# Attention over head pairs: both parts of the values in one stationary operand, halves of the result added on VectorE

## The chip, the cores and the metric

The kernel runs on one core of a Trainium2 chip. The metric is the device time of one execution in microseconds, as the median of several runs. In the profile PE is TensorE's matmuls and PEld its weight loads, DVE is VectorE, ACT is ScalarE, POOL is GpSimd, SP is SyncE, which here issues all transfers.

## The reference

Two layers, each an attention and a feed-forward part, work on 16 batches of 256 tokens with 512 features. Only the attention of the first layer is touched:

```
q = (x @ Wq).reshape(B, N, HEADS, DIM_HEAD)          # 16 heads of 64
out    = attend(q, ctx_txt @ Wk,    ctx_txt @ Wv)    # context rows 0..76
out_ip = attend(q, ctx_img @ Wk_ip, ctx_img @ Wv_ip) # context rows 77..255
return (out + out_ip) @ Wo + bo
# attend: softmax(q k^T / 8) @ v, for each head
```

Here x is the normalized input. The two softmaxes run over different columns of one 256x256 score matrix, and since their results are added, one product of the probabilities (both parts scaled by their own sums) with all 256 value rows gives out + out_ip.

## The kernel before

All products are made from float32r operands in two parts: a high part, and a low part that is what the high part leaves of the float32 value. `product` (lines 186 to 192) issues three matmuls: high x high, high x low and low x high.

The changed function is `attend_pairs`. It works through N = 128 head pairs (16 batches x 8 pairs). It is a software pipeline written out as Python loops: each engine has its own list, and in step s of the list it does its share of several pairs at different stages. The lists are strictly in order; semaphores tie them together. In step s, TensorE does:

- `scores(s)`: eight matmuls of 128x256 into the score tile `sc[s % 2]`, two banks with four blocks (two heads x two query tiles);
- `turn(s - 2)`: eight transposes of the probabilities into `tp`;
- `turn_output`, in one step of four: four transposes of a finished, normalized output tile, into the score tile of the pair before;
- `values(s - 3)`: for each of two heads and two key tiles a `product` into `vq[:, 0]`, twelve matmuls of 128x256. The stationary operand `vs` is 128 columns wide, of which one head's values fill 64 and zeros the others, so that both heads add up in one tile of 128 rows;
- `queries(s + 3)`: twelve matmuls of 128x256 into `vq[:, 1]`, the other half of the same bank;
- `project_out`: six matmuls of 128x512 for two pairs of an output tile, `LAG_O` steps behind; in one step of four a bias matmul comes ahead of them (line 1013).

ScalarE makes the exponentials (`exps`, line 910, in two groups of columns: 77 text and 179 image), the high part of the transposed probabilities (`turned_high`, line 923), of the keys (`keys_high`, line 917), and of outputs and queries in one go (`high_parts`, lines 929 and 933). VectorE finds the row maxima (`largest`, line 802), the sums (`totals`, line 808) and their reciprocals, and the low parts of probabilities (`turned_low`, line 819), outputs and queries (`low_parts`, lines 825 and 827). For each finished output tile, one in four steps, it adds the residual (`output`, line 853) and takes the statistics (lines 833 to 837). GpSimd scales the probabilities (`normalize`, line 773), makes the keys' low part (line 760) and places both parts of the values into `vs` (`place_values`, lines 753 and 755). SyncE's queue loads keys and values and stacks the queries' parts (`stack_q`), four transfers a pair.

## Time and profile before

| | |
|---|---|
| median of 3 runs | 3418.91 us (3418.05 to 3422.42) |
| profiled execution, span | 3417.2 us |
| TensorE busy over the span | 3209.3 us (94%) |
| VectorE, ScalarE, GpSimd busy | 1912.3, 1553.2, 780.6 us |
| `attend_pairs` | about 455 to 1280 us of the span |

The changed part takes a quarter of the span. For it one reads the busy time of each engine inside that stretch, not over the whole span, then the timeline of single steps, and then the list of who waited for whom. Busy time counts overlapping instructions once: an engine's next instruction often starts before the last has ended, so what one adds to a full list is its distance from start to start, which is less than its own length.

### The profile page before, as it was taken

Reading aid. Unit: us, or ns where it says so; the run is one execution under the profiler, and the core shown is the slowest. Engines: PE = TensorE matmul, PEld = TensorE weight load, DVE = VectorE, ACT = ScalarE, POOL = GpSimd, SP = SyncE. Lnnn points to the kernel's source line nnn. Section 1 sums busy time; section 2 is a strip of 40 time slices with the busy share of each in tenths; the row PEclk is TensorE's granted clock in tenths of the full one; section 3 lists DMA queues with packets and bytes.
Section 4 is the critical chain, followed back from the end, with each engine's and each line's share of the span. In section 5 each row is a group of like instructions: output and inputs, shape, how many; then the busy total and the mean of one; then the engine's idle time right before and its main releaser. Section 6 shows DMA issues by size and latency. Waiting matters only on the chain. (4 is left out here: it accounts for less than half of the span.)

```text
span 3417.2 us, 51469 instructions
## 1 busy us (share of the span) xinstructions
PE 3209.3 (94%) x17304; PEld 2753.0 (81%) x17304; DVE 1912.3 (56%) x3294; ACT 1553.2 (45%) x2948; POOL 780.6 (23%) x1138
## 2 busy tenths in 40 slices
PE   7999979999999988999996888997979999999998
PEld 6989969999999986887875576886857888888886
DVE  3244558888888874556888996554753222222211
ACT  3122247777777753335766786654731111111110
POOL 0000047777777750000000200002710000000000
...
GB/s 186 125 250 235 212 184 146 164 163 159 156 157 160 154 96 239 191 175 188 216 226 222 195 275 229 160 161 161 259 117 74 37 35 19 22 37 38 31 25 13
DMA packets 370164, 503.48 MB, mean 147 GB/s; under 512 B 58940, under 2 KB 237420, under 8 KB 366032
## 3 DMA queue, kind: packets, MB, share of 16 engines
...
q8 instruction: 127, 2.08, 0.3%
...
## 5 line engine op out<-in xcount | busy, mean ns | idle before, releaser
L2571 DVE SCALAR_TENSOR_TENSOR lf_hT<-lf_hb,lf_hT 128x512 fp32r<-128x512 f32 x128 | 88.6, 692 | 571.4 <-ACT lf_hT L2647 571.4
L2647 ACT ACTIVATE lf_hT<-lf_hb 128x512 fp32r<-128x512 f32 x128 | 76.6, 599 | 669.1 <-PE lf_py L192 639.6
L910 ACT ACTIVATE at_prob<-at_sc,at_nm 128x77 f32<-128x77 f32 (+1 forms) x1024 | 292.7, 382 | 3.4 <-DVE at_nm L802 3.4
L773 POOL TENSOR_TENSOR at_prob<-at_prob,at_rec 128x308 f32<-128x308 f32 (+1 forms) x256 | 261.6, 1044 | 136.8 <-DVE at_rec L815 136.8
L802 DVE TENSOR_REDUCE at_nm<-at_sc 128x4 f32<-128x308 f32 (+1 forms) x256 | 164.7, 685 | 80.2 <-PE at_sc L965 80.0
L190 PE MATMUL lf_hb<-lf_xT,lf_w 128*128 128x512 f32 x512 | 204.5, 400 | 1.3 <-DVE lf_hT L2571 1.3
L192 PE MATMUL lf_hb<-lf_xT,lf_w 128*128 128x512 f32 x512 | 203.6, 398 | 0.0
L192 PE MATMUL lf_py<-lf_w,lf_hT 128*128 128x512 f32 x512 | 203.4, 397 | 0.0
L190 PE MATMUL lf_py<-lf_w,lf_hT 128*128 128x512 f32 x512 | 203.2, 397 | 0.0
L191 PE MATMUL lf_hb<-lf_xT,lf_w 128*128 128x512 f32 x512 | 203.1, 397 | 0.0
L191 PE MATMUL lf_py<-lf_w,lf_hT 128*128 128x512 f32 x512 | 202.7, 396 | 0.0
L923 ACT ACTIVATE at_pT<-at_tp 128x1024 fp32r<-128x1024 f32 x128 | 131.4, 1027 | 155.7 <-PE at_tp L975 155.7
L2500 POOL TENSOR_SCALAR lf_var<-lf_mv 128x1 f32<-128x1 f32 x32 | 7.4, 230 | 717.6 <-DVE lf_mv L2523 717.6
L190 PE MATMUL pg_bank<-qu_xs,qg_wg 128*128 128x512 f32 x384 | 153.2, 399 | 16.4 <-DVE qu_xs L1396 16.4
L760 POOL TENSOR_TENSOR at_ks<-at_kr,at_ks 128x512 fp32r<-128x512 f32 x128 | 165.0, 1289 | 9.4 <-ACT at_ks L917 9.4
L190 PE MATMUL dn_py<-qf_wd,dn_om 128*128 128x512 f32 x384 | 150.8, 393 | 16.0 <-DVE dn_om L1917 16.0
L808 DVE TENSOR_REDUCE at_sums<-at_prob 128x4 f32<-128x308 f32 (+1 forms) x256 | 162.5, 676 | 0.0
L190 PE MATMUL at_vq<-at_xT,xo_Wq 128*128 128x256 f32 x512 | 146.6, 286 | 13.9 <-DMA at_xT<-xn_parts 11.9
L190 PE MATMUL pu_bank<-qu_xs,qu_wu 128*128 128x512 f32 x384 | 150.8, 393 | 8.5 <-SPq L1270 5.7
L190 PE MATMUL at_vq<-at_pT,at_vs 128*128 128x256 f32 x512 | 154.8, 302 | 0.0
L819 DVE TENSOR_TENSOR at_pT<-at_tp,at_pT 128x1024 fp32r<-128x1024 f32 x128 | 152.7, 1193 | 2.8 <-ACT at_pT L923 2.7
L191 PE MATMUL pg_bank<-qu_xs,qg_wg 128*128 128x512 f32 x384 | 150.7, 392 | 0.0
...
## 6 DMA issues: line engine op xcount, KB each, us to landing
at_kr<-k_rows SPq DMA_DIRECT2D x256, 128.0 KB, 2.9
at_qs<-at_qst SPq DMA_DIRECT2D x512, 64.0 KB, 2.1
...
```

What stands on the lines that cost most here:

```text
L190: pe.matmul(out, lh, rh, start=start, stop=False, **kw)
L191: pe.matmul(out, lh, rl, start=False, stop=False, **kw)
L192: return pe.matmul(out, ll, rh, start=False, stop=stop, **kw)
L760: pool.tensor_tensor(ks[:, n % NK, :, 1, :], kr[:, n % NKR], ks[:, n % NK, :, 0, :].bitcast(F32), ALU.subtract).then_inc(k_low, 1)
L773: ins = pool.tensor_tensor(prob[:, i, :, lo:hi], prob[:, i, :, lo:hi], rec[:, z, g, :].unsqueeze(2).broadcast_to([P, 2 * NTE, hi - lo]), A ...
L802: ins = dve.tensor_reduce(nm[:, n % 2, g, :], sc[n % 2][:, :, lo:hi], AX_X, ALU.max, negate=True)
L808: dve.tensor_reduce(sums[:, z, g, :], prob[:, i, :, SEG[g][0]:SEG[g][1]], AX_X, ALU.add).then_inc(sum_done, 1)
L819: dve.tensor_tensor(pT[:, n % 2, 1], tp[:], pT[:, n % 2, 0].bitcast(F32), ALU.subtract).then_inc(pt_done, 1)
L910: ins = act.activation(prob[:, i, m, lo:hi], sc[n % 2][:, m, lo:hi], ACT.Exp, bias=nm[:, n % 2, g, m:m + 1])
L923: act.activation(pT[:, n % 2, 0], tp[:], ACT.Copy).then_inc(pt_hi, 1)
L2571: dve.scalar_tensor_tensor(hT[:, i, 1, :], hb[i][:], 0.0, hT[:, i, 0, :].bitcast(F32), ALU.max, ALU.subtract).then_inc(h_done, 1)
L2647: act.activation(hT[:, m % 2, 0, :], hb[m % 2][:], ACT.Relu).then_inc(h_hi, 1)
```

## The change

- `vs` becomes `[P, NVP, NTE, 2, 2, DH]`: for a head and a key tile, 64 columns of high parts and 64 of low parts lie side by side, and are one stationary operand of 128 columns. `values` issues, for each head and key tile, two matmuls with it, against the high and the low part of the probabilities: eight instead of twelve. Rows 0 to 63 of the result hold the products with the high part of the values, rows 64 to 127 those with the low part (low x low among them, which was left out before). No zeros are kept any more, and their memset goes.
- The result goes to half of a score tile (`attended(s)`, the first two blocks of `sc[(s + 1) % 2]`), one block of 256 columns for each head. ScalarE copies rows 64 to 127 to `corr` (`corrections`), VectorE adds them to rows 0 to 63 and writes `osum`, head 0 to partitions 0 to 63 and head 1 to 64 to 127 (`halves_summed`).
- From `osum` ScalarE makes the outputs' high part (`outputs_high`) and GpSimd the low part (`outputs_low`), one step later than before.
- The values' high part is made by ScalarE (`values_high`), the low part by GpSimd in one instruction (`values_low`).
- Queries have a bank of their own (`qb`) and come first in TensorE's step. `scores` and `values` wait for `o_summed`, and `values` also for the exponentials of the pair before, whose tile they write.
- `LAG_O` grows from 8 to 9, and the lists of ScalarE, VectorE and GpSimd have a new order.

The core of the diff:

```diff
     NTE = S // P
     N = B * NPAIR
-    LAG_T, LAG_V, LEAD_Q, LAG_P = 2, 3, 3, 2
+    LAG_T, LAG_V, LEAD_Q = 2, 3, 3
     LEAD_K, LEAD_KH, LEAD_KL = 5, 3, 2
-    LAG_O = NPAIR
+    LAG_H, LAG_S = 1, 4
+    LAG_O = NPAIR + 1
...
-        vs = ph.sb("vs", [P, NVP, 2, NTE, 2, P], F32R)
+        vs = ph.sb("vs", [P, NVP, NTE, 2, 2, DH], F32R)
...
+        corr = ph.sb("corr", [DH, 2, S])
+        osum = ph.sb("osum", [P, 2, S])
...
-        vq = ph.ps("vq", [P, 2, S])
+        qb = ph.ps("qb", [P, 2 * S])
...
+        def attended(s):
+
+            return sc[(s + 1) % 2][:, 0:NTE, :]
...
-                    if 0 < s < N and s % 2 == 0:
-                        load_v(s // 2)
+                    if 0 < s + 1 < N and s % 2:
+                        load_v((s + 1) // 2)
...
-                def place_values(n, part):
+                def values_low(n):
                     g, l = n // 2, n % 2
-                    if part == 0:
-                        pool.wait_ge(v_ready[g % 2], 16 * (g // 2 + 1))
-                        if n >= NVP:
-                            pool.wait_ge(vq_full, v_count(n - NVP))
-                    else:
-                        pool.wait_ge(v_high, n + 1)
-                    for h in range(2):
-                        lo = DH * h
-                        to, src = vs[:, n % NVP, h, :, :, lo:lo + DH], vr[:, g % 2, :, l * P + lo:l * P + lo + DH]
-                        if part == 0:
-                            ins = pool.tensor_copy(to[:, :, 0, :], src)
-                        else:
-                            ins = pool.tensor_tensor(to[:, :, 1, :], src, to[:, :, 0, :].bitcast(F32), ALU.subtract)
-                    ins.then_inc(v_high if part == 0 else v_placed, 1)
+                    pool.wait_ge(v_high, n + 1)
+                    pool.tensor_tensor(vs[:, n % NVP, :, :, 1, :], vr[:, g % 2, :, l * P:(l + 1) * P].rearrange("p k (h d) -> p k h d", d=DH),
+                                       vs[:, n % NVP, :, :, 0, :].bitcast(F32), ALU.subtract).then_inc(v_placed, 1)
+
+                def outputs_low(n):
+                    pool.wait_ge(o_hi, n + 1)
+                    pool.tensor_tensor(oT[:, n % NO, 1, :], osum[:, n % 2, :], oT[:, n % NO, 0, :].bitcast(F32), ALU.subtract).then_inc(o_low, 1)
...
-                    if 0 <= s - LAG_P < N:
-                        place_values(s - LAG_P, 0)
                     if 0 <= s + LEAD_KL < N:
                         keys_low(s + LEAD_KL)
-                    if 0 <= s - LAG_P < N:
-                        place_values(s - LAG_P, 1)
                     if 0 <= s - 1 < N:
                         normalize(s - 1)
+                    if 0 <= s - LAG_S < N:
+                        outputs_low(s - LAG_S)
+                    if 0 <= s - LAG_H < N:
+                        values_low(s - LAG_H)
...
-                def low_parts(s):
-                    n, m = s - LAG_V, s + LEAD_Q
-                    dve.wait_ge(vq_hi, s + LEAD_Q + 1)
-                    if 0 <= n < N:
-                        ins = dve.tensor_tensor(oT[:, n % NO, 1, :], vq[:, 0, :], oT[:, n % NO, 0, :].bitcast(F32), ALU.subtract)
-                    if m < N:
-                        ins = dve.tensor_tensor(qst[:, m % NQS, 1, :], vq[:, 1, :], qst[:, m % NQS, 0, :].bitcast(F32), ALU.subtract)
-                    ins.then_inc(vq_done, 1)
+                def halves_summed(s):
+                    n = s - LAG_V
+                    dve.wait_ge(corr_out, n + 1)
+                    if n >= 2:
+                        dve.wait_ge(o_low, n - 1)
+                    for h in range(2):
+                        ins = dve.tensor_tensor(osum[DH * h:DH * h + DH, n % 2, :], attended(s)[0:DH, h, :], corr[:, h, :], ALU.add)
+                    ins.then_inc(o_summed, 1)
+
+                def queries_low(m):
+                    dve.wait_ge(q_hi, m + 1)
+                    dve.tensor_tensor(qst[:, m % NQS, 1, :], qb[:, 0:S], qst[:, m % NQS, 0, :].bitcast(F32), ALU.subtract).then_inc(q_done, 1)
...
+                    if out_tile(s - 1):
+                        output(*out_tile(s - 1))
+                    if 0 <= s - 1 < N:
+                        totals(s - 1, 0)
+                        totals(s - 1, 1)
+                        reciprocals(s - 1)
+                    if out_tile(s - 3):
+                        row_maximum(*out_tile(s - 3))
                     if 0 <= s < N:
                         largest(s)
-                    if 0 <= s - 1 < N:
-                        totals(s - 1, 0)
-                    if 0 <= s - 1 < N:
-                        totals(s - 1, 1)
-                        reciprocals(s - 1)
-                    if out_tile(s - 1):
-                        output(*out_tile(s - 1))
+                    if s + LEAD_Q < N:
+                        queries_low(s + LEAD_Q)
+                    if 0 <= s - LAG_V < N:
+                        halves_summed(s)
                     if out_tile(s - 2):
                         offset(*out_tile(s - 2))
                     if 0 <= s - LAG_T < N:
                         turned_low(s - LAG_T)
-                    if out_tile(s - 3):
-                        row_maximum(*out_tile(s - 3))
-                    if s < N + LAG_V:
-                        low_parts(s)
                     if out_tile(s - 1):
...
-                def high_parts(s):
-                    n, m = s - LAG_V, s + LEAD_Q
-                    act.wait_ge(vq_full, s + LEAD_Q + 1)
-                    if 0 <= n < N:
-                        ins = act.activation(oT[:, n % NO, 0, :], vq[:, 0, :], ACT.Copy)
-                    if m < N:
-                        if m >= NQS:
-                            act.wait_ge(q_ready[(m - NQS) % NQ], 64 * ((m - NQS) // NQ + 1))
-                        ins = act.activation(qst[:, m % NQS, 0, :], vq[:, 1, :], ACT.Copy)
-                    ins.then_inc(vq_hi, 1)
+                def values_high(n):
+                    g, l = n // 2, n % 2
+                    act.wait_ge(v_ready[g % 2], 16 * (g // 2 + 1))
+                    if n >= NVP:
+                        act.wait_ge(v_full, n - NVP + 1)
+                    act.activation(vs[:, n % NVP, :, :, 0, :], vr[:, g % 2, :, l * P:(l + 1) * P].rearrange("p k (h d) -> p k h d", d=DH), ACT.Copy
+                                   ).then_inc(v_high, 1)
+
+                def corrections(s):
+                    n = s - LAG_V
+                    act.wait_ge(v_full, n + 1)
+                    if n:
+                        act.wait_ge(o_summed, n)
+                    act.activation(corr[:], attended(s)[DH:P], ACT.Copy).then_inc(corr_out, 1)
+
+                def outputs_high(n):
+                    act.wait_ge(o_summed, n + 1)
+                    act.activation(oT[:, n % NO, 0, :], osum[:, n % 2, :], ACT.Copy).then_inc(o_hi, 1)
+
+                def queries_high(m):
+                    act.wait_ge(q_full, m + 1)
+                    if m >= NQS:
+                        act.wait_ge(q_ready[(m - NQS) % NQ], 64 * ((m - NQS) // NQ + 1))
+                    act.activation(qst[:, m % NQS, 0, :], qb[:, 0:S], ACT.Copy).then_inc(q_hi, 1)
...
+                    if 0 <= s - LAG_S < N:
+                        outputs_high(s - LAG_S)
+                    if s + LEAD_Q < N:
+                        queries_high(s + LEAD_Q)
+                    if 0 <= s + LEAD_KH < N:
+                        keys_high(s + LEAD_KH)
                     if 0 <= s - LAG_T < N:
                         turned_high(s - LAG_T)
+                    if 0 <= s - LAG_V < N:
+                        corrections(s)
+                    if 0 <= s - LAG_H < N:
+                        values_high(s - LAG_H)
                     if out_tile(s - 3):
                         turned_output(*out_tile(s - 3), s)
                     if 0 <= s < N:
                         exps(s, 0)
-                    if 0 <= s + LEAD_KH < N:
-                        keys_high(s + LEAD_KH)
-                    if s < N + LAG_V:
-                        high_parts(s)
+                        exps(s, 1)
                     if out_tile(s - 2):
                         normalized(*out_tile(s - 2))
-                    if 0 <= s < N:
-                        exps(s, 1)
...
+                    if n > LAG_V:
+                        pe.wait_ge(o_summed, n - LAG_V)
...
-                def values(n):
+                def values(s):
+                    n = s - LAG_V
                     pe.wait_ge(v_placed, n + 1)
                     pe.wait_ge(pt_done, n + 1)
+                    pe.wait_ge(exp_done, 2 * min(s, N))
+                    if n >= 2:
+                        pe.wait_ge(o_summed, n - 1)
                     for h in range(2):
                         for k in range(NTE):
-                            ins = product(pe, vq[:, 0, :], (vs[:, n % NVP, h, k, 0, :], vs[:, n % NVP, h, k, 1, :]),
-                                          (pT[:, n % 2, 0, k, h * S:(h + 1) * S], pT[:, n % 2, 1, k, h * S:(h + 1) * S]),
-                                          h == 0 and k == 0, h == 1 and k == NTE - 1)
-                    return ins
+                            for part in range(2):
+                                ins = pe.matmul(attended(s)[:, h, :], vs[:, n % NVP, k, h, :, :].rearrange("p a d -> p (a d)"),
+                                                pT[:, n % 2, part, k, h * S:(h + 1) * S], start=k == 0 and part == 0, stop=k == NTE - 1 and part == 1)
+                    ins.then_inc(v_full, 1)
...
+                    if n:
+                        pe.wait_ge(q_done, n)
...
-                        ins = product(pe, vq[:, 1, :], (wq[:, 0, lo:lo + P], wq[:, 1, lo:lo + P]), (xT[:, b % 2, 0, k, :], xT[:, b % 2, 1, k, :]),
+                        ins = product(pe, qb[:, 0:S], (wq[:, 0, lo:lo + P], wq[:, 1, lo:lo + P]), (xT[:, b % 2, 0, k, :], xT[:, b % 2, 1, k, :]),
                                       k == 0, k == KD - 1)
-                    return ins
+                    ins.then_inc(q_full, 1)
...
-                        ins = pe.transpose(sc[(s + 1) % 2][:, k * P // S, k * P % S:k * P % S + P],
+                        ins = pe.transpose(sc[(s + 1) % 2][:, NTE + k * P // S, k * P % S:k * P % S + P],
...
-                            pe.wait_ge(vq_done, v_count(n))
+                            pe.wait_ge(o_low, n + 1)
...
+                    if s + LEAD_Q < N:
+                        queries(s + LEAD_Q)
...
-                    if s < N + LAG_V:
-                        if s > FIRST:
-                            pe.wait_ge(vq_done, s + LEAD_Q)
-                        if 0 <= s - LAG_V:
-                            ins = values(s - LAG_V)
-                        if s + LEAD_Q < N:
-                            ins = queries(s + LEAD_Q)
-                        ins.then_inc(vq_full, 1)
+                    if 0 <= s - LAG_V < N:
+                        values(s)
```

In TensorE's list, at a plain step of the steady part, stands before (the three rows of `at_vq<-at_pT` come four times, then those of `at_vq<-at_xT` four times, then the projection):

```order
L965 MATMUL at_sc<-at_ks,at_qs 128x256 x8
L975 MATMUL at_tp<-ident,at_prob 128x128 x8
L190 MATMUL at_vq<-at_pT,at_vs 128x256
L191 MATMUL at_vq<-at_pT,at_vs 128x256
L192 MATMUL at_vq<-at_pT,at_vs 128x256
```

and now (ahead of these rows the three query rows come four times, the projection behind them twice):

```order
L190 MATMUL at_qb<-at_xT,xo_Wq 128x256
L191 MATMUL at_qb<-at_xT,xo_Wq 128x256
L192 MATMUL at_qb<-at_xT,xo_Wq 128x256
L984 MATMUL at_sc<-at_ks,at_qs 128x256 x8
L994 MATMUL at_tp<-ident,at_prob 128x128 x8
L1007 MATMUL at_sc<-at_pT,at_vs 128x256 x8
L190 MATMUL at_pj<-xo_Wo,at_oT 128x512
```

The queries moved ahead of the scores, and eight value matmuls into `at_sc` stand where twelve into `at_vq` did.

VectorE's list, one plain step; `at_sc0` and `at_sc1` are the two score tiles. Before:

```order
L802 TENSOR_REDUCE at_nm<-at_sc1 128x4 x2
L808 TENSOR_REDUCE at_sums<-at_prob 128x4 x2
L815 RECIPROCAL at_rec<-at_sums 128x8
L819 TENSOR_TENSOR at_pT<-at_tp,at_pT 128x1024
L825 TENSOR_TENSOR at_oT<-at_vq,at_oT 128x256
L827 TENSOR_TENSOR at_qst<-at_vq,at_qst 128x256
```

Now:

```order
L801 TENSOR_REDUCE at_sums<-at_prob 128x4 x2
L808 RECIPROCAL at_rec<-at_sums 128x8
L795 TENSOR_REDUCE at_nm<-at_sc0 128x4 x2
L825 TENSOR_TENSOR at_qst<-at_qb,at_qst 128x256
L820 TENSOR_TENSOR at_osum<-at_sc1,at_corr 64x256 x2
L812 TENSOR_TENSOR at_pT<-at_tp,at_pT 128x1024
```

The totals of the pair before moved ahead of the maxima, the queries' low part ahead of the probabilities' low part, and the two additions stand between them.

ScalarE's list, one plain step. Before:

```order
L910 ACTIVATE at_prob<-at_sc0,at_nm 128x179 x4
L923 ACTIVATE at_pT<-at_tp 128x1024
L910 ACTIVATE at_prob<-at_sc1,at_nm 128x77 x4
L917 ACTIVATE at_ks<-at_kr 128x2x256
L929 ACTIVATE at_oT<-at_vq 128x256
L933 ACTIVATE at_qst<-at_vq 128x256
```

Now:

```order
L940 ACTIVATE at_oT<-at_osum 128x256
L946 ACTIVATE at_qst<-at_qb 128x256
L915 ACTIVATE at_ks<-at_kr 128x2x256
L921 ACTIVATE at_pT<-at_tp 128x1024
L936 ACTIVATE at_corr<-at_sc0 64x512
L928 ACTIVATE at_vs<-at_vr 128x4x64
L908 ACTIVATE at_prob<-at_sc1,at_nm 128x77 x4
L908 ACTIVATE at_prob<-at_sc1,at_nm 128x179 x4
```

The copy of the transposed probabilities moved from ahead of the exponentials' text part to the middle of the step, the two groups of exponentials stand together at its end, and behind the probabilities' copy come the new copies of corrections and values.

## Rows read from the trace of the kernel before

**Rows 1.** The page's first line: the profiled execution.
```profile
span 3417.2 us, 51469 instructions
```

**Rows 2.** Busy us and instructions of PE, PEld, DVE, ACT, POOL; PEclk, DMA, GB/s.
```profile
700.00:800.00 100.00, 100.00 (x759) 95.73 (x758) 81.84 (x153) 73.14 (x202) 75.69 (x117) 1.00 0.54 158
```

**Rows 3.** Timeline of PE in one step: start, us long, what, how many.
```profile
804.42 0.40 PE L190 MATMUL at_pj<-xo_Wo,at_oT 128*128 128x512 f32 x1
...
805.81 1.11 PE L965 MATMUL at_sc<-at_ks,at_qs 128*128 128x256 f32 x8
806.76 1.04 PE L975 MATMUL at_tp<-ident,at_prob 128*128 128x128 f32 x8
807.55 0.36 PE L190 MATMUL at_vq<-at_pT,at_vs 128*128 128x256 f32 x1
807.75 0.28 PE L191 MATMUL at_vq<-at_pT,at_vs 128*128 128x256 f32 x1
...
809.06 0.28 PE L190 MATMUL at_vq<-at_xT,xo_Wq 128*128 128x256 f32 x1
...
812.11 1.11 PE L965 MATMUL at_sc<-at_ks,at_qs 128*128 128x256 f32 x8
```

**Rows 4.** Waits, 600 to 1200 us: who for whom, sum, times, longest.
```profile
POOL at_prob L773 <- DVE at_rec L815: 103.2, 72, 1.9
DVE at_nm L802 <- PE at_sc L965: 64.3, 72, 0.9
...
DVE at_oT L825 <- ACT at_qst L933: 33.8, 72, 0.6
```

**Rows 5.** Timeline of DVE in a step with an output tile.
```profile
806.96 1.29 DVE L802 TENSOR_REDUCE at_nm<-at_sc 128x4 f32<-128x308 f32 x2 [0.89 <-PE at_sc L965]
...
809.59 0.64 DVE L853 TENSOR_TENSOR at_y<-at_pj,at_y 128x512 f32<-128x512 f32 x1
810.14 1.22 DVE L819 TENSOR_TENSOR at_pT<-at_tp,at_pT 128x1024 fp32r<-128x1024 f32 x1
811.39 0.42 DVE L825 TENSOR_TENSOR at_oT<-at_vq,at_oT 128x256 fp32r<-128x256 f32 x1
811.74 0.41 DVE L827 TENSOR_TENSOR at_qst<-at_vq,at_qst 128x256 fp32r<-128x256 f32 x1
812.07 0.68 DVE L833 BATCH_NORM_STATS2 at_st<-at_y 128x6 f32<-128x512 f32 x1
...
813.30 1.28 DVE L802 TENSOR_REDUCE at_nm<-at_sc 128x4 f32<-128x308 f32 x2
```

**Rows 6.** Timeline of ACT, two stretches of the steady part.
```profile
804.90 0.38 ACT L933 ACTIVATE at_qst<-at_vq 128x256 fp32r<-128x256 f32 x1
805.16 1.32 ACT L910 ACTIVATE at_prob<-at_sc,at_nm 128x179 f32<-128x179 f32 x4
...
821.14 0.59 ACT L901 ACTIVATE at_xt<-at_sc 128x512 f32<-128x512 f32 x1
821.62 0.98 ACT L910 ACTIVATE at_prob<-at_sc,at_nm 128x77 f32<-128x77 f32 x4
822.45 0.67 ACT L917 ACTIVATE at_ks<-at_kr 128x512 fp32r<-128x512 f32 x1
```

**Rows 7.** Groups of POOL, 600 to 1200 us: busy us, mean ns, idle before.
```profile
L760 POOL TENSOR_TENSOR at_ks<-at_kr,at_ks 128x512 fp32r<-128x512 f32 x97 | 125.0, 1289 | 0.0
...
L755 POOL TENSOR_TENSOR at_vs<-at_vr,at_vs 128x128 fp32r<-128x128 f32 x192 | 84.4, 461 | 0.0
...
L753 POOL CAST at_vs<-at_vr 128x128 fp32r<-128x128 f32 x192 | 50.9, 294 | 0.0
```

**Rows 8.** Timeline of PE in the first steps: scores and transposes of one step.
```profile
485.36 1.12 PE L965 MATMUL at_sc<-at_ks,at_qs 128*128 128x256 f32 x8
486.70 1.09 PE L975 MATMUL at_tp<-ident,at_prob 128*128 128x128 f32 x8 [0.23 <-POOL at_prob L773]
...
490.51 1.12 PE L965 MATMUL at_sc<-at_ks,at_qs 128*128 128x256 f32 x8
```

21 lines of the change are left out of this document (8 added, 13 removed).

## The prediction

> **What bounds the kernel now.** I read the busy shares of each engine by stretch first. In the attention stage TensorE is busy for all of 100 us in 100, at granted clock 1.00, while VectorE has 82, GpSimd 76 and ScalarE 73 [rows 2]. Next comes the timeline of TensorE: a step (one head pair) begins with its scores, and the next scores begin 6.30 us later (805.81 to 812.11), with no idle time between them [rows 3]. The waits of 600 us in the steady part name the other engines as waiting, never TensorE [rows 4]. So a TensorE column removed here is time removed, as long as the others keep up. They are what has to be costed.
>
> That step has a bias matmul, which every fourth one has; of 128x512 each costs 0.23 ((805.81 - 804.42)/6), so a plain step is 6.07 us. Another one of four has four output transposes, 0.4 us by the (807.55 - 806.76)/8 = 0.1 of the others [rows 3]. That makes 6.07 + 0.63/4 = 6.23 us on average. By this, VectorE has 0.818 x 6.23 = 5.10 us of work in a step, ScalarE 0.731 x 6.23 = 4.56, GpSimd 0.757 x 6.23 = 4.72.
>
> **TensorE.** The twelve value matmuls (two heads, two key tiles, three products) become eight: one stationary operand holds 64 columns of high and 64 of low parts, and gets the two parts of the probabilities. A further matmul of 128x256 costs 0.12 us start to start: from 807.75 to 809.06 there are eleven, 0.119 each [rows 3]. Four fewer are 0.476 us a step, and 128 steps give **61.0 us**. Bounds of the new form: its output goes to a score bank instead of vq, but the score matmuls, which write there, take (806.76 - 805.81)/8 = 0.119 too. I take that. The order queries, scores, transposes, values, projection has as many changes of kind as before, so I cost the move at nothing. The new step is 6.23 - 0.48 = 5.75 us.
>
> **ScalarE.** It loses nothing and gains two copies. The correction copy (64x512 out of PSUM) is nearest to the turned output, 128x512 out of PSUM: 0.59 us long, 0.48 before the next starts. Half the partitions could halve it, at best 0.24. The high part of the values (128x256, SBUF) is nearest to the keys' copy, 128x512 in 0.67 [rows 6], and to the queries' copy of 256 columns, 0.26 start to start [rows 6]: I take 0.30, at worst 0.67. The other copies keep their size. Sum 4.56 + 0.48 + 0.30 = 5.34, bounds 5.1 and 5.8: over TensorE's 5.75 only at the worst end.
>
> **VectorE.** It loses the output's low part, 0.35 start to start (811.39 to 811.74), and gains two additions of 64x256 from PSUM and SBUF. The nearest row is that same subtraction, 0.42 long, 0.35 apart; half the partitions might cost half, 0.18 [rows 5]. I take 0.35 each, as the time of the rows goes with the columns: sum 5.10 - 0.35 + 0.70 = 5.45. If they and the instruction behind them get no overlap, it is 5.10 - 0.35 + 0.84 + 0.10 = 5.69; at half the cost, 5.10. All are under 5.75, the upper one by 1%.
>
> [...] The second addition writes from partition 64 on, and the turned_low behind it from 0 on. [...] No row here shows an output that starts at 64. [...]
>
> **GpSimd and the queue.** GpSimd loses two casts (50.9/96 = 0.53 a pair) and two low parts (84.4/96 = 0.88) [rows 7] and gains two subtractions of 128x256, each half of the keys' 1.29 [rows 7]: 4.72 - 1.41 + 1.30 = 4.61, and 5.07 if each costs what the old pair did. It is no bound, and its longest step, the scaling of the probabilities, feeds a transposition two steps later. On SyncE's queue only the load of values moves, by one step; its wait, for values placed a step before, is met by then. stack_q waits for the queries' low part as before, and its result is needed three steps later.
>
> **The new waits.** (a) The values now use the score bank of the pair before, so scores(s+1) wait for halves_summed(s). Behind the last value matmul come 0.2 us until its result is seen, the copy 0.6 [rows 6], two additions 0.84 [rows 5] and handoffs of 0.1, together about 1.75. TensorE has the projection (1.40) and the twelve query matmuls (1.43) to do meanwhile, 2.83 [rows 3]: slack 1.1. (b) queries(s+3) begin the step and wait for the previous queries' low part, which on VectorE stands behind totals, reciprocal and largest. In a plain step the values end at 4.2 us after the step's start, the correction copy at 5.05, the additions at 5.9, turned_low (1.1, 810.14 to 811.39 less its wait [rows 5]) at 7.0. The exponentials, which follow ScalarE's two new copies, run from 5.25 to 7.4 (0.83 + 1.3 [rows 6]); then come totals and reciprocal to 8.5, largest to 9.75 (with the first totals the three take 2.63, 806.96 to 809.59 [rows 5]) and the low part to 10.15. TensorE wants it at 11.3, slack 1.1. After a step with statistics (1.23 from 812.07 to 813.30 [rows 5]) it comes at 11.3 and is wanted at 11.4. That is the tightest place, at 0.1 us, once in four steps. (c) turn(s-1) waits for turned_low(s-2): done at 7.1, wanted at 8.0, and late by about the same in the step after the statistics. I cost all three at nothing; their cover is TensorE's own work, and every 0.1 us of missing cover costs 32 x 0.1 = 3.2 us at (b).
>
> **Start and end.** In the first steps there is no projection, and a step takes 5.15 us (485.36 to 490.51), TensorE waiting for GpSimd's scaling [rows 8]. There the removed matmuls give nothing: five pairs x 0.48 = 2.4 us off the gain. LAG_O + 1 takes one pair's projection (1.40) out of step 8, which becomes 5.15 instead of 5.60, and puts it behind the last values: 1.40 - 0.45 = 0.9 more. Together 3.3 us lost.
>
> **Sum.** 61.0 - 3.3 = 57.7 us gained. Against the profiled span of 3417.2 us [rows 1] that is 3359.5; the median of the runs lies 1.7 above that span, so **3361 us**.
>
> **The rivals.**
> 1. VectorE is late at (b) and (c) after each statistics step. For it: slack 0.1 there, and its waits for ScalarE's copies, 33.8 us in 96 steps [rows 4]. Against it: three of four steps have a microsecond to spare. If 0.5 us is missing a time, 32 x 0.5 = 16 us: 3377.
> 2. VectorE bounds every step. Its upper sum 5.69 plus the 0.35 a step that it now waits for ScalarE (33.8/96) is 6.04, a gain of 0.19 x 128 = 24 less 3: 3398. It needs both at their worst.
> 3. The other side: the lists lock into one ring. Values(s), correction copy, values' copy, both exponentials, totals with reciprocal and largest, queries' low part, additions, and scores, transposes and values two steps on are 0.6 + 0.3 + 0.8 + 1.3 + 2.6 + 0.4 + 0.8 + 2.7, with handoffs 10 us over two steps, against 11.5 that TensorE gives them. It costs time from 12.5 on, the old two steps: the VectorE work of a tile (output 0.64, statistics 1.23 [rows 5]) would have to fall into the ring each time, and its waits for scores (64.3/96 = 0.67 a step [rows 4]) stay as well. Then a step is 5.69 + 0.35 + 0.67 = 6.7, 128 x 0.47 = 60 us slower: 3479.
> 4. The change doesn't do what it says: the new matmuls take 0.179 each, as long as twelve at 0.119. Then 3419 + 3 = 3422. Only the score matmuls speak, and against it.
>
> **How the numbers follow.** Forecast (3355 to 3369) 0.63; first rival (3369 to 3386) 0.18; second (3386 to 3411) 0.09; a small remainder within 0.2% of before, rival 4 among it, 0.04; slower by the ring 0.06. A difference under 0.2% (7 us) is one that these runs can't tell from none. The range has to hold 0.8 and takes in the forecast, the first rival and the lower part of the second: 3355 to 3394. Faster by over 0.2%: 0.63 + 0.18 + 0.09 = 0.90; same 0.04; slower 0.06.
>
> **What would show it.** In the profile after: eight value matmuls a pair at 0.12 us start to start; 100 us in 100 for TensorE from about 510 us on; 5.6 us from scores to scores in plain steps and 5.75 on average; no wait of TensorE's query matmuls for VectorE; VectorE near 95% and ScalarE near 93%. The sum is wrong if TensorE has idle time in front of its queries or transposes once in four steps (rival 1), in each step (rival 2), or in front of its scores, ended by the additions (rival 3).

## The result and the profile after

The changed kernel takes **3376.44 us** (median of 4 runs, 3373.63 to 3377.83) where the kernel before, run beside it, took 3420.66 (4 runs, 3418.05 to 3425.37): ratio 0.9871, 95% interval 0.9859 to 0.9883, 44 us less. The forecast was 3361 with a range of 3355 to 3394; its own narrow case ended at 3369. So direction and range held. The narrow case did not: of the 57.7 us expected, 44.2 came by the medians run side by side. The profiled execution's span fell from 3417.2 [rows 1] to 3375.4, by 41.8, so there 15.9 are missing. From here on a pair is numbered 0 to 127, and scores(5) are the score matmuls of pair 5.

The page's first line, as [rows 1]:

```profile
span 3375.4 us, 51188 instructions
```

The stretch of [rows 2], in the changed kernel (busy us and instructions of PE, PEld, DVE, ACT, POOL; then granted clock, DMA share, GB/s):

```profile
700.00:800.00 100.00, 100.00 (x745) 94.46 (x744) 94.98 (x182) 94.20 (x249) 83.28 (x91) 1.00 0.59 174
```

TensorE still has no idle time there, at granted clock 1.00. VectorE and ScalarE went from 82 and 73 to 95 and 94. One step of TensorE, as [rows 3], with the start of the step behind it:

```profile
801.89 1.12 PE L984 MATMUL at_sc<-at_ks,at_qs 128*128 128x256 f32 x8
...
803.64 1.19 PE L1007 MATMUL at_sc<-at_pT,at_vs 128*128 128x256 f32 x8
804.67 0.39 PE L190 MATMUL at_pj<-xo_Wo,at_oT 128*128 128x512 f32 x1
...
806.08 0.39 PE L190 MATMUL at_qb<-at_xT,xo_Wq 128*128 128x256 f32 x1
806.30 0.28 PE L191 MATMUL at_qb<-at_xT,xo_Wq 128*128 128x256 f32 x1
...
807.61 1.12 PE L984 MATMUL at_sc<-at_ks,at_qs 128*128 128x256 f32 x8
...
813.65 1.12 PE L984 MATMUL at_sc<-at_ks,at_qs 128*128 128x256 f32 x8
...
819.25 1.12 PE L984 MATMUL at_sc<-at_ks,at_qs 128*128 128x256 f32 x8
...
825.08 1.12 PE L984 MATMUL at_sc<-at_ks,at_qs 128*128 128x256 f32 x8
```

The eight value matmuls take 1.03 us (803.64 to 804.67) where the twelve took 1.51 [rows 3]. The plain step, from 813.65 on, takes 5.60, and four steps 23.19 (801.89 to 825.08), 5.80 each where 5.75 was expected. One thing was not expected: the first query matmul at 806.08 is followed after 0.22 us instead of 0.12. The waits of the steady part say why (who for whom, sum in us, times, longest), as [rows 4]:

```profile
PEld at_qb L190 <- DVE at_qst L825: 7.8, 25, 0.6
...
PE at_sc L984 <- DVE at_osum L820: 0.7, 2, 0.4
```

Once in four steps (25 times in some 104) the weight load of the queries waits for the low part of the queries before (L825). It is wait (b) of the prediction. It doesn't show as idle time of PE, since the load (0.19 us from 806.07) overlaps the last projection matmul (0.39 us from 805.83); it shows as a first matmul that is 0.1 us longer.

**Where the span went.** I cut the stage at four events that every kernel has: its first query matmul; the start of scores(9); the start of the very last score matmul (the eighth of pair 127); and the first matmul of the next stage (pg_bank). What was expected of each piece follows from the prediction's own terms, with 0.476 us a pair: six pairs' values lie ahead of scores(9), 119 between, three behind.

| us (profiled executions) | before | after | gain | gain expected | missing |
|---|---|---|---|---|---|
| first queries to scores(9) | 55.9 | 61.6 | -5.7 | 6 x 0.476 - 2.4 + 0.45 = 0.9 | 6.6 |
| scores(9) to the last score matmul | 736.0 | 683.6 | 52.4 | 119 x 0.476 = 56.6 | 4.2 |
| last score matmul to the next stage | 46.9 | 52.3 | -5.4 | 3 x 0.476 - 1.4 = 0 | 5.4 |

Together 16.2 us are missing, which is the whole difference of the spans from the forecast (3375.4 against 3359.5) to 0.3. The runs below had to find the cause of each of the three. Their rows and this table come from one execution of each kernel. The steady piece repeats well: in the four profiles whose steady part has the changed kernel's code it is 683.6 to 683.9 (changed, k0, k2, k5 below). The first piece varies by several us between executions, as will be seen, and so does what lies outside the stage: 455.1 to 460.9 us ahead of it and 2118.7 to 2124.5 behind it in the fourteen profiles. A gain of 3 us at one end can therefore drown in a median.

### The profile page after: what moved, and what is told of

Same layout as the page of the kernel before. It is cut to its first block and busy times, and to the rows that moved or that the text cites. A ratio compares the mean times of both kernels' runs of the same rounds, so it can differ in the third digit from the quotient of the medians.

```text
span 3375.4 us, 51188 instructions
## 1 busy us (share of the span) xinstructions
PE 3161.2 (94%) x16792; PEld 2696.3 (80%) x16792; DVE 1962.9 (58%) x3422; ACT 1667.3 (49%) x3204; POOL 789.5 (23%) x881
## 5 line engine op out<-in xcount | busy, mean ns | idle before, releaser
L908 ACT ACTIVATE at_prob<-at_sc,at_nm 128x77 f32<-128x77 f32 (+1 forms) x1024 | 277.6, 385 | 7.3 <-DVE at_nm L795 4.9
L190 PE MATMUL at_qb<-at_xT,xo_Wq 128*128 128x256 f32 x512 | 151.5, 296 | 23.4 <-DVE at_qst L825 12.0
L812 DVE TENSOR_TENSOR at_pT<-at_tp,at_pT 128x1024 fp32r<-128x1024 f32 x128 | 156.3, 1221 | 3.3 <-ACT at_pT L921 0.3
L190 PE MATMUL pu_bank<-qu_xs,qu_wu 128*128 128x512 f32 x384 | 151.2, 394 | 7.1 <-SPq L1291 5.6
L1007 PE MATMUL at_sc<-at_pT,at_vs 128*128 128x256 f32 x1024 | 153.1, 292 | 1.4 <-issue 1.4
L191 PE MATMUL pu_bank<-qu_xs,qu_wu 128*128 128x512 f32 x384 | 150.6, 392 | 0.0
```

The lines of the kernel that those rows point to most:

```text
L190: pe.matmul(out, lh, rh, start=start, stop=False, **kw)
L191: pe.matmul(out, lh, rl, start=False, stop=False, **kw)
L812: dve.tensor_tensor(pT[:, n % 2, 1], tp[:], pT[:, n % 2, 0].bitcast(F32), ALU.subtract).then_inc(pt_done, 1)
L908: ins = act.activation(prob[:, i, m, lo:hi], sc[n % 2][:, m, lo:hi], ACT.Exp, bias=nm[:, n % 2, g, m:m + 1])
L1007: ins = pe.matmul(attended(s)[:, h, :], vs[:, n % NVP, k, h, :, :].rearrange("p a d -> p (a d)"), pT[:, n % 2, part, k, h * S:(h + 1) * S] ...
```

## The experiments

All medians are in us, each with the ratio to the kernel before run on the same chip and its 95% interval. The columns "start", "steady" and "tail" are the three pieces of the table above.

| kernel | median | ratio | start | steady | tail |
|---|---|---|---|---|---|
| changed | 3376.44 | 0.9871 [0.9859, 0.9883] | 61.6 | 683.6 | 52.3 |
| k0: changed, again | 3376.79 | 0.9874 [0.9857, 0.9890] | 58.0 | 683.9 | 52.4 |
| k3: twelve matmuls | 3430.18 | 1.0035 [1.0021, 1.0049] | 62.4 | 735.5 | 54.3 |
| k1: low part ahead | 3369.84 | 0.9858 [0.9842, 0.9875] | 58.4 | 680.6 | 52.6 |
| k4: sums in the same half | 3372.46 | 0.9870 [0.9853, 0.9886] | 59.2 | 679.7 | 51.8 |
| k12: k1 and k4 | 3367.68 | 0.9845 [0.9831, 0.9858] | 58.4 | 679.3 | 52.2 |
| k8: k1, turned_low first | 3382.17 | 0.9887 [0.9870, 0.9903] | 58.5 | 691.5 | 52.0 |
| k2: scores first at the start | 3379.96 | 0.9891 [0.9875, 0.9908] | 60.9 | 683.9 | 52.8 |
| k5: turned_low first in the tail | 3378.47 | 0.9871 [0.9854, 0.9887] | 58.3 | 683.7 | 50.7 |
| k7: k1 and k5 | 3369.78 | 0.9853 [0.9837, 0.9870] | 55.8 | 680.7 | 52.0 |
| k6: k1, k2 and k5 | 3377.67 | 0.9875 [0.9858, 0.9891] | 61.7 | 680.6 | 52.2 |
| k9: k1, lead of two | 3370.21 | 0.9854 [0.9838, 0.9870] | 54.8 | 681.1 | 52.8 |
| k11: k9 and k5, end reordered | 3367.54 | 0.9846 [0.9833, 0.9860] | 54.8 | 681.2 | 49.0 |

### Is it the four matmuls? (k3)

The matmul with the low part of the probabilities is issued twice.

```
-  for part in range(2):
-      pe.matmul(..., pT[:, n % 2, part, k, ...], start=k == 0 and part == 0, stop=k == NTE - 1 and part == 1)
+  for i, part in enumerate((0, 1, 1)):
+      pe.matmul(..., pT[:, n % 2, part, k, ...], start=k == 0 and i == 0, stop=k == NTE - 1 and i == 2)
```

> The changed kernel, but the value matmul with the low part of the probabilities is issued twice, so that twelve value matmuls a pair are there again (the result counts that part twice and is not the reference's). Theory: the whole gain comes from the four matmuls, and what is left is what the new order costs at the start and the end: a step of 6.23 us, no waits at the queries, 61 us more less some 8 that TensorE now waits: 3429 us, 9 us over the kernel before. Rival: the new order by itself gained, or VectorE holds the pace in part; then it is under 3415.

Measured: 3430.18 us, ratio 1.0035 [1.0021, 1.0049]. Timeline of PE, the value matmuls and what follows:

```profile
799.95 1.67 PE L1007 MATMUL at_sc<-at_pT,at_vs 128*128 128x256 f32 x12
801.46 0.40 PE L190 MATMUL at_pj<-xo_Wo,at_oT 128*128 128x512 f32 x1
```

Twelve of the new form take 1.51 us, as the twelve of the old did. The steady piece is 735.5 against 736.0 before: with twelve matmuls to cover them, the new operand, the moved work, the copies and additions cost nothing there, and the four matmuls are the whole gain. What this kernel loses to the one before, about 11 us, lies at the two ends: its start is 6.5 and its tail 7.4 longer. So the ends cost something even when no matmul is removed.

### The steady part: wait (b) (k1)

The queries' low part moves ahead of `largest` in VectorE's order.

```
-  if 0 <= s < N:
-      largest(s)
   if s + LEAD_Q < N:
       queries_low(s + LEAD_Q)
+  if 0 <= s < N:
+      largest(s)
```

> The changed kernel with one edit on VectorE's list: queries_low(s + 3) stands ahead of largest(s) instead of behind it. Theory: TensorE's queries are late because their release waits behind the maxima. In the steady part that cost about 0.035 us a step (4 us in all), in the first steps about 0.8 us each (TensorE idle 0.8 before the queries of steps 3 to 7). Both go: 3376.4 - 4 - 4 = 3368 us, and no wait of the queries for VectorE in the steady part. Rival: the loss is VectorE's and ScalarE's added work, whatever its order: 3376 within 2 us, the wait moves to the scores or the transposes.

Measured: 3369.84 us, 0.9858 [0.9842, 0.9875]; all its runs (3367.43 to 3371.87) lie under all of the changed kernel's. The intervals of the two ratios overlap, but the same difference comes back where both were run side by side: k9, which has this edit, took 3368.98 to 3371.93, and k0, which has not, 3374.82 to 3377.80. Its waits of 600 to 1200 us hold no wait of PE or PEld at at_qb any more:

```profile
ACT at_prob L908 <- DVE at_nm L795: 5.8, 26, 0.6
...
PE at_sc L984 <- DVE at_osum L820: 1.8, 3, 1.2
```

The steady piece is 680.6 instead of 683.6 (683.9 in the second execution). Thirty statistics steps at 0.1 us are the 3.0 us. The price went to an engine that can bear it: ScalarE now waits 5.8 us for `largest`. Of the 4.2 missing, 3.0 are thereby shown. The rest, 1.2, lies within the last three scores of the piece (below, 0.38, 0.30 and 1.16 us). The median moved by more than 3 us, 6.6, and the piece at the start moved too; how much of that is this edit is taken up with the start.

### The steady part: the distances of the additions (k4, k12)

The second addition of halves writes partitions 64 to 127 of osum, its neighbours start at 0. To see whether that takes overlap from them, it writes here a tile of its own, at partition 0, and the upper half of osum is set to zero once (not shown), so that the result is not the reference's.

```
+  aside = ph.sb("aside", [DH, 2, S])
...
   for h in range(2):
-      dve.tensor_tensor(osum[DH * h:DH * h + DH, n % 2, :], ...)
+      dve.tensor_tensor((osum if h == 0 else aside)[0:DH, n % 2, :], ...)
```

> The changed kernel, but the addition of the second head writes to partitions 0 to 63 of a tile aside instead of 64 to 127 of osum, which are left at zero (the output is not the reference's). [...] Rival: additions on 64 partitions have no overlap anyway (the wait for the copy, or the two inputs): distances and time as in the changed kernel, 3376.

Measured: 3372.46 us (3369.47 to 3375.02), 0.9870 [0.9853, 0.9886]. The time as a whole can't be told from the changed kernel's (3373.63 to 3377.83, 0.9871); what follows rests on the profile. Timeline of DVE in the changed kernel:

```profile
811.66 0.84 DVE L820 TENSOR_TENSOR at_osum<-at_sc,at_corr 64x256 f32<-64x256 f32 x2
812.54 1.22 DVE L812 TENSOR_TENSOR at_pT<-at_tp,at_pT 128x1024 fp32r<-128x1024 f32 x1
```

and in this one:

```profile
806.77 0.42 DVE L825 TENSOR_TENSOR at_osum<-at_sc,at_corr 64x256 f32<-64x256 f32 x1
807.12 0.41 DVE L825 TENSOR_TENSOR at_aside<-at_sc,at_corr 64x256 f32<-64x256 f32 x1
807.45 1.21 DVE L815 TENSOR_TENSOR at_pT<-at_tp,at_pT 128x1024 fp32r<-128x1024 f32 x1
```

From the first addition to turned_low it is 0.88 us in the one (811.66 to 812.54) and 0.68 in the other (806.77 to 807.45). The two additions overlap their followers, as the subtraction of 128x256 does in [rows 5], only in k4: with all outputs at partition 0 the distances are 0.35 and 0.33 us, for additions of 0.42 and 0.41; with the second output at 64 they are 0.42 and 0.46, 0.07 and 0.13 more. So additions on 64 partitions do overlap, and the rival is out. The prediction's upper sum for VectorE, 5.69, had 0.84 + 0.10 us for these distances. The wait at the queries goes here too, and the steady piece becomes 679.7, 3.9 less, where equal code repeats within 0.3. So the same 3 to 4 us of the steady part can be had from either end of the wait. Both at once, as k1 and k4 together,

> The changed kernel with queries_low ahead of largest, and the second head's addition writing to partitions 0 to 63 of a tile aside (osum's upper half is zero, the output is not the reference's). Theory: what VectorE loses to the change of partitions costs time only where TensorE waits for VectorE; the first edit took that wait away, so the 4 us that the second gave alone come once, not twice: 3369 within 1.5 us. Rival: the two gains add up, as VectorE's pace sets the step: 3365 or less.

measured 3367.68 us (5 runs, 3364.02 to 3372.71), 0.9845 [0.9831, 0.9858], with a steady piece of 679.3. In that piece the gains do not add: once the wait is gone, more room on VectorE is worth 1.3 us over 119 pairs.

### The steady part: the slack of wait (a) (k8)

To see whether the additions have the 1.1 us of slack that the prediction gave them, turned_low (1.1 us) is put ahead of them, on top of the edit of k1.

```
+  if 0 <= s - LAG_T < N:
+      turned_low(s - LAG_T)
   if 0 <= s - LAG_V < N:
       halves_summed(s)
   ...
-  if 0 <= s - LAG_T < N:
-      turned_low(s - LAG_T)
```

> The changed kernel with queries_low ahead of largest, and turned_low ahead of the additions in all steps. It takes the slack of the scores' new wait, which I had put at 1.1 us: the additions now end some 1.1 us later. Theory: TensorE waits for them at the scores in the steps with little slack, some 0.1 to 0.5 us a step, so 10 to 50 us slower than with the first edit alone: 3380 to 3420. Rival: the additions have slack to spare (VectorE's list only turns two entries that both come in time), and the time stays at 3370, or 3367 with the shorter end.

Measured: 3382.17 us, 0.9887 [0.9870, 0.9903], 12.3 above k1; the steady piece 691.5 against 680.6, 0.09 us a pair. The waits, 600 to 1200 us:

```profile
PEld at_sc L984 <- issue: 7.2, 27, 1.7
...
PE at_sc L984 <- DVE at_osum L820: 2.2, 4, 1.3
```

The delay of 1.1 us is nearly all absorbed. What is left comes mostly once in four steps: in 23 of the 27 cases the weight load of the scores is 0.16 to 0.18 us late, and the longest, 1.7, belongs to the last scores. The profile names no releaser for it; the traces show that it is the additions. From the end of the second addition to the start of the scores that wait for it, k1 has 1.0 to 1.3 us in three of four steps and 0.7 in the fourth, and this kernel 0.15 in two of four and 0.3 and 0.5 in the others. So the slack was about 1.1 as costed in the plain steps and a little less in one of four. The loop from values over additions to scores did not set the pace, or 1.1 us more in it would have cost 65 us (1.1 us in every two steps) up to 130 (in each). Of rival 2 the run says nothing, since it leaves the amount of VectorE's work as it was.

### The start (k0, k2, k9)

The timeline of PE in the first 20 us of the stage, changed kernel (the bracket is idle time before, and what ended it; left out are further query matmuls):

```profile
460.62 0.58 PE L190 MATMUL at_qb<-at_xT,xo_Wq 128*128 128x256 f32 x1 [0.93 <-DVE at_qst L825]
461.00 0.41 PE L191 MATMUL at_qb<-at_xT,xo_Wq 128*128 128x256 f32 x1
461.21 0.41 PE L192 MATMUL at_qb<-at_xT,xo_Wq 128*128 128x256 f32 x1
...
464.48 0.58 PE L190 MATMUL at_qb<-at_xT,xo_Wq 128*128 128x256 f32 x1 [0.93 <-DVE at_qst L825]
...
471.06 1.84 PE L984 MATMUL at_sc<-at_ks,at_qs 128*128 128x256 f32 x8
```

and in the kernel before:

```profile
460.58 0.39 PE L190 MATMUL at_vq<-at_xT,xo_Wq 128*128 128x256 f32 x1 [0.93 <-DVE at_qst L827]
...
463.20 0.39 PE L190 MATMUL at_vq<-at_xT,xo_Wq 128*128 128x256 f32 x1 [0.93 <-DVE at_qst L827]
...
465.74 1.21 PE L965 MATMUL at_sc<-at_ks,at_qs 128*128 128x256 f32 x8 [0.84 <-DMA at_qs<-at_qst]
```

Two things differ. Since queries now stand first in a step, four groups of them come ahead of scores(0) instead of three, and scores(0) starts 5.3 us later (471.06 against 465.74). And the clock: the query matmuls are 0.21 us apart all through, at a granted clock of 0.50 (460 to 471 us), where before they were 0.12 apart from the second group on, at 1.00 (461 to 466 us). A group therefore lasts 3.86 us (460.62 to 464.48) instead of 2.62 (460.58 to 463.20). The granted clock is the seventh column, for 456 to 486 us, first of the kernel before:

```profile
456.00:486.00 30.00, 22.34 (x150) 20.83 (x151) 15.33 (x26) 16.23 (x46) 16.20 (x22) 0.87 0.64 189
```

of the changed one:

```profile
456.00:486.00 30.00, 22.19 (x108) 20.56 (x109) 10.16 (x20) 11.83 (x33) 11.10 (x10) 0.61 0.63 184
```

and of a second job with the same changed kernel:

```profile
456.00:486.00 30.00, 22.57 (x140) 20.69 (x140) 12.63 (x24) 15.11 (x43) 13.13 (x12) 0.81 0.69 192
```

> The changed kernel as it is, on the same chip and in the same rounds as the last variant, so that the differences of the variants are not put down to chips. Both theories: 0.9871 of the kernel before, within 0.0015.

Measured: 3376.79 us, 0.9874 [0.9857, 0.9890]. Its profiled execution was at clock 1.00 from the third group of queries on (0.50 up to 464 us, 1.00 for 466 to 476) and had scores(9) after 58.0 us instead of 61.6, and yet its median is the same. So 3.6 of the 6.6 us missing at the start belong to one execution. The fourth group, 2.6 us at clock 1.00, is about the rest: scores(0) come 11.9 us after the first queries in k0 and came after 9.0 before the change, 2.9 later, while scores(0) to scores(9) take 46.1 in k0 and took 46.9. In steps 4 to 8 the changed kernel looks like this:

```profile
490.84 0.38 PE L190 MATMUL at_qb<-at_xT,xo_Wq 128*128 128x256 f32 x1 [0.83 <-DVE at_qst L825]
...
492.37 1.12 PE L984 MATMUL at_sc<-at_ks,at_qs 128*128 128x256 f32 x8
...
497.56 1.12 PE L984 MATMUL at_sc<-at_ks,at_qs 128*128 128x256 f32 x8
```

Without a projection to run, TensorE waits 0.7 to 0.8 us at its queries in each step: the step is 5.2, as long as before ([rows 8], 5.15), so little is lost, but what ends the wait is (b) and no longer GpSimd.

Can the start be had back? In k2 the first four steps keep the old order.

```
-  if s + LEAD_Q < N:
+  if s >= 4 and s + LEAD_Q < N:
       queries(s + LEAD_Q)
   ...
       values(s)
+  if s < 4:
+      queries(s + LEAD_Q)
```

> The changed kernel with one edit on TensorE's list: in steps before 4 the queries come behind scores and values, as in the kernel before; from step 4 on ahead. Theory: scores(0) began 5.3 us later than before (471.06 against 465.74) because queries(3) and their wait stood ahead of them; scores(0) goes back to about 466 us and the kernel gains 2 to 5 us: 3373. Steady part unchanged. Rival (the first steps are bound by the longer lists of the other engines): scores(0) begins at 466, but scores(6) still at 503, and the time stays 3376.

Measured: 3379.96 us, 0.9891 [0.9875, 0.9908], 3.5 above the changed kernel where 3 less were expected. A miss. Timeline of PE where the order changes back:

```profile
480.11 1.12 PE L984 MATMUL at_sc<-at_ks,at_qs 128*128 128x256 f32 x8
483.52 1.94 PE L994 MATMUL at_tp<-ident,at_prob 128*128 128x128 f32 x8 [2.30 <-DVE at_pT L812]
485.12 1.93 PE L1007 MATMUL at_sc<-at_pT,at_vs 128*128 128x256 f32 x8
...
489.40 0.38 PE L190 MATMUL at_qb<-at_xT,xo_Wq 128*128 128x256 f32 x1 [0.93 <-DVE at_qst L825]
...
491.96 1.18 PE L984 MATMUL at_sc<-at_ks,at_qs 128*128 128x256 f32 x8 [0.87 <-DVE at_osum L820]
```

Up to scores(3) at 480.11 it keeps the order of the kernel before. Then one step takes 11.9 us (480.11 to 491.96): the transposes wait 2.3 us for turned_low, since the queries that covered it are elsewhere, the granted clock is 0.50 behind that gap (483.4 to 485 us), where the eight transposes take 1.60 us (483.52 to 485.12) instead of 0.79 [rows 3], and two groups of queries stand in a row with wait (b) between them. What the start order gained, the changeover gave back. A lead of two pairs instead of three, on top of k1, has no changeover.

```
-  LAG_T, LAG_V, LEAD_Q = 2, 3, 3
+  LAG_T, LAG_V, LEAD_Q = 2, 3, 2
...
-  FIRST, LAST = -LEAD_Q, N + LAG_O + 3
+  FIRST, LAST = -LEAD_Q - 1, N + LAG_O + 3
...
-  if s + LEAD_Q < N:
+  if 0 <= s + LEAD_Q < N:
```

> The changed kernel with queries_low ahead of largest, and with LEAD_Q = 2 on all lists: the queries still come first in TensorE's step, but for two steps ahead instead of three, so that scores(0) wait for three groups of queries, not for four. Theory: with four groups the start loses one round of queries, high part, low part (3.86 us between the first query groups); k1's scores(5) began 37.8 us after the first query, now 34; the steady part keeps its pace, since the stacked queries had a step to spare; the last steps have queries to cover the additions one step longer. 3369.8 - 4 = 3366 us. Rival: the stacking transfers are late with one step less and scores wait for them in every step (slower than 3376), or the start is bound by the ring of additions and scores alone (3370).

Measured: 3370.21 us, 0.9854 [0.9838, 0.9870]. In its profiled execution scores(9) come after 54.8 us, earlier than before the change and 3.6 earlier than k1's; the median is k1's. But most of the 3.6 is the clock of k1's execution, whose four groups were all at 0.50 (up to 471 us). k7 (below) has the same start, four groups and all, was at 1.00 from the third group on (from 464 us), and reached scores(9) after 55.8. Against k7, leaving out the fourth group saves 1.0, too little to be seen in a median; k9 was at 0.50 through three groups (up to 468 us) and k7 through two, which hides part of the 2.6.

The same pairs show what k1's edit gives at the start. Where scores(0) come equally late, scores(9) come 3.3 us sooner with it (k1 58.4, changed 61.7; scores(0) after 14.3 in both) and 2.2 sooner (k7 55.8, k0 58.0; 11.9 in both). Counted from scores(0) on, which leaves out the first groups, the kernels with it take 43.9 to 44.3 us (k1, k7, k9, k11, k12) and those without 45.1 (k5), 46.1 (k0) and 47.3 (changed). So wait (b) costs 1 to 3 us at the start besides the 3.0 of the steady part, which makes 4 to 6 of the 6.6 by which k1's median is lower.

### The tail (k5, k7, k6, k11)

From scores(125) on there are no queries left to run between values and scores. The changed kernel's PE there:

```profile
1190.04 1.18 PE L984 MATMUL at_sc<-at_ks,at_qs 128*128 128x256 f32 x8 [0.38 <-DVE at_osum L820]
...
1195.23 1.18 PE L984 MATMUL at_sc<-at_ks,at_qs 128*128 128x256 f32 x8 [0.30 <-DVE at_osum L820]
...
1201.04 1.19 PE L984 MATMUL at_sc<-at_ks,at_qs 128*128 128x256 f32 x8 [1.16 <-DVE at_osum L820]
...
1207.77 1.06 PE L994 MATMUL at_tp<-ident,at_prob 128*128 128x128 f32 x8 [1.53 <-DVE at_pT L812]
...
1212.84 1.06 PE L994 MATMUL at_tp<-ident,at_prob 128*128 128x128 f32 x8 [1.53 <-DVE at_pT L812]
```

Wait (a) opens three times, and then the transposes wait twice for turned_low, wait (c), for 1.53 us: the step is 5.07 (1207.77 to 1212.84). Behind them TensorE waits 1.35 us for its values at 1217.82 and 1.35 for the normalised output at 1221.75. Leaving aside the last three waits, which both kernels have alike, TensorE stands 5.9 us behind its last scores where it stood 1.24 before the change (the first row below); that is most of the 5.4 missing. A step of the tail before:

```profile
1253.84 1.09 PE L975 MATMUL at_tp<-ident,at_prob 128*128 128x128 f32 x8 [1.24 <-POOL at_prob L773]
...
1257.82 1.04 PE L975 MATMUL at_tp<-ident,at_prob 128*128 128x128 f32 x8
```

In k5 turned_low goes ahead of the additions in the steps after the last scores only.

```
+  if s >= N and 0 <= s - LAG_T < N:
+      turned_low(s - LAG_T)
   if 0 <= s - LAG_V < N:
       halves_summed(s)
   ...
-  if 0 <= s - LAG_T < N:
+  if not (s >= N) and 0 <= s - LAG_T < N:
       turned_low(s - LAG_T)
```

> The changed kernel with one edit on VectorE's list, in its last steps only (s >= 128): turned_low ahead of the additions. Theory: behind the last scores TensorE waits 1.53 us twice for turned_low, which stands behind the additions, which wait for the values of the same step; 5.6 us were lost there against the kernel before. Two waits of 1.5 go: 3 us less, 3373 or 3374. Rival: the end is bound by the longer way of the last outputs (copy, addition, high part, low part, projection); then nothing changes.

Measured: 3378.47 us (3371.39 to 3379.80), 0.9871 [0.9854, 0.9887]: the profile's tail is 1.6 shorter, where 3 were expected, and the median shows nothing. With k1's edit beside it, and with all three edits:

> As the kernel with all three edits, without the one on the start (queries ahead from the first step on, as in the changed kernel). Theory: 3369.8 less 3 for the end: 3367. With the kernel of three edits it tells what the order of the first four steps is worth.

> The changed kernel with three edits: queries_low ahead of largest; queries behind the values in steps before 4; turned_low ahead of the additions in the last steps. Theory: 6.6 from the first, as measured, 3 from the last; the second alone lost the 4 us it had gained once the order changed at step 4, because the queries' release stood behind the maxima; with that gone it may keep 2: 3365 to 3367. Rival: the start is bound by the ring of copy, additions and scores: the second gives nothing and the time equals that without it.

Measured: 3369.78, 0.9853 [0.9837, 0.9870], which is k1's own time; and 3377.67, 0.9875 [0.9858, 0.9891], which takes k1's gain back, as the changeover at the start did in k2 (its steady piece is k1's, 680.6, its start 61.7). The two were run side by side and differ in the order of the first four steps alone: 7.9 us, 5.9 of them in the profile's start. Both missed. Why the tail gained so little is in k7's PE:

```profile
1210.95 0.85 PE L1029 MATMUL at_sc<-ident,at_xn 128*128 128x128 f32 x4 [1.91 <-ACT at_xn L894]
...
1212.02 0.63 PE L191 MATMUL at_pj<-xo_Wo,at_oT 128*128 128x512 f32 x1
```

Its second wait for turned_low is gone (0.52 us for GpSimd instead of 1.53), the values come earlier, and then TensorE waits 1.91 us for the normalised output (at_xn) ahead of the output transposes. Behind that gap the projection matmuls are 0.43 us apart (1212.02, and 0.63 long instead of 0.40, six of them) instead of 0.23, at a granted clock of 0.50 (1212 to 1214 us). The wait had only moved on. It is the wait that k5 has too, and there the clock behind it stayed at 1.00 (1221 to 1224 us):

```profile
1220.76 0.66 PE L1029 MATMUL at_sc<-ident,at_xn 128*128 128x128 f32 x4 [1.91 <-ACT at_xn L894]
...
1221.49 0.39 PE L191 MATMUL at_pj<-xo_Wo,at_oT 128*128 128x512 f32 x1
```

That is the difference between k7's tail of 52.0 and k5's of 50.7, 1.3 us: the gap took a part of the expected 3 us in both, the clock another part in k7 alone. So the last version puts the output transposes behind the projection in the last steps, on top of k9 and k5.

```
-  if out_tile(s - 3):
+  if s < N and out_tile(s - 3):
       turn_output(*out_tile(s - 3), s)
   ...
       project_out(*out_part(s))
+  if s >= N and out_tile(s - 3):
+      turn_output(*out_tile(s - 3), s)
```

> The changed kernel with queries_low ahead of largest, LEAD_Q = 2, turned_low ahead of the additions in the last steps, and in those steps TensorE's output transposes behind the projection instead of ahead of the values. Theory: the edit of VectorE's list alone gained nothing at the end because TensorE then stood 1.91 us before the output transposes, and the clock fell to its lower level for the matmuls behind it; with the transposes behind the projection neither comes: the end is 3 us shorter (last scores to next stage 49.5 us instead of 52.3): 3367. Rival: the end is bound by the output tile's own chain of addition, statistics, power, shift and normalization, whatever TensorE does in between: 3370.

Measured: 3367.54 us (5 runs, 3362.55 to 3369.43), 0.9846 [0.9833, 0.9860]. The wait is 0.55 now, and the matmuls behind it are at clock 1.00 (1212 to 1214 us), which after k5 can't be put down to the shorter gap:

```profile
1211.65 0.66 PE L1029 MATMUL at_sc<-ident,at_xn 128*128 128x128 f32 x4 [0.55 <-ACT at_xn L894]
...
1212.38 0.39 PE L191 MATMUL at_pj<-xo_Wo,at_oT 128*128 128x512 f32 x1
```

The tail is 49.0 against 52.8 in k9. All five runs lie below all four of the changed kernel. Against k9 the intervals overlap, so that the 2.7 us of the tail's edits alone are likely and not shown.

## Why the prediction was right, and where it was off

**The range held, in part by luck.** The time lies outside the forecast's own case (3355 to 3369) and inside the bracket of the first rival (3369 to 3386), which the range took in. As shown below, that rival's mechanism paid the smaller part of what is missing, and the rest was not among the rivals.

**TensorE's gain: right.** The term of 61.0 us was four matmuls at 0.119. k3 and the table show it at its size: steady piece 735.5 with twelve, 680.6 with eight and no wait (b), 54.9 of the 56.6 costed; the last three scores' waits for the additions (0.38 + 0.30 + 1.16 = 1.8) make up the rest. Rival 4 (0.179 each) is out: 1.03 us for eight. That the average step is 5.80 and not 5.75 has two reasons: from scores(20) to scores(120) the old step was 6.25 and not 6.23, and 0.03 is wait (b).

**Engines.** VectorE is 0.950 x 5.80 = 5.51 us a step against the 5.45 taken and the 5.69 of its upper sum. Up to turned_low the pair of additions took 0.88 us instead of 0.70, near the 0.94 of that sum; 5.10 - 0.35 + 0.88 is 5.63, so that another part was some 0.1 too high. ScalarE is 0.942 x 5.80 = 5.46 against 5.34: its two new copies last until the next one for 0.49 and 0.43, where I had taken 0.48 and 0.30 (timeline of ACT, changed kernel):

```profile
804.98 0.60 ACT L936 ACTIVATE at_corr<-at_sc 64x512 f32<-64x512 f32 x1
805.47 0.41 ACT L928 ACTIVATE at_vs<-at_vr 128x256 fp32r<-128x256 f32 x1
805.90 2.17 ACT L908 ACTIVATE at_prob<-at_sc,at_nm 128x77 f32<-128x77 f32 x8
```

GpSimd is 0.833 x 5.80 = 4.83 against 4.61: a subtraction of 128x256 costs 0.74, not half of 1.29 (groups of 600 to 1200 us: busy us, mean ns, idle before):

```profile
L746 POOL TENSOR_TENSOR at_vs<-at_vr,at_vs 128x256 fp32r<-128x256 f32 x103 | 76.3, 740 | 0.0
```

None of them reached TensorE's step of 5.80, which was the claim.

**Wait (a): right** in the steady part (k8), wrong in the last three steps, where its cover, the query matmuls, no longer exists. **Wait (b): right in place, off in size.** It was called the tightest, at 0.1 us of slack once in four steps. The slack was slightly under zero: 0.1 us late each time, 3.0 us in all. In the other steps it was smaller than costed as well: from the end of the queries' low part to the first query matmul the changed kernel has 0.5 to 0.7 us, not 1.1. By the prediction's own price ("every 0.1 us of missing cover costs 32 x 0.1 = 3.2 us") it is rival 1 at a fifth of its size; rival 1's total of 3377 was met, but its mechanism paid 3 of the 16 missing us. At the start, where no projection covers it, the same wait costs another 1 to 3. Of the signs that were named, "no wait of TensorE's query matmuls for VectorE" is one that failed: the weight load waits for it in the steady part, and TensorE itself in the first steps. **Wait (c): right** in the steady part, where no such wait shows, wrong in the tail, twice 1.5 us.

**Start and end: the term that was mis-sized.** It was costed at 3.3 us, and the first and last rows of the table come to that plus 12.0 in the profiled execution (6.6 + 5.4), plus 8.5 in that of k0 (3.0 + 5.5). I had counted there the gain that can't be made and the projection that moves, and not that the new waits lose their cover at both ends (queries at the end, projection at the start), nor that one query group more stands ahead of scores(0), nor that the granted clock can be 0.50 through more of the first groups. The trace of before has the rows for the first two, its first steps and its last ones. The clock it could not have told, as it differs between two executions of one kernel.

**Rivals 2 and 3: out.** TensorE is busy 100 of 100 us in the stretch, so neither VectorE nor the ring sets the pace, and 1.1 us more in the ring costs 0.09 us a pair (k8).

**What stays open.** The start differs by up to 3.6 us between two executions of the same kernel, and the kernel before has one profile only. So the share of the missing 16 us that belongs to the start is known as 3 to 7 us, no closer. Why the clock is at 1.00 from the third group of queries on in k0 and at 0.50 through four groups in the other execution of the same kernel is not shown, nor why it fell to 0.50 behind the gap in k7 and not in k5.
